# Attention features as sixteen 32x32 TensorE tiles over head pairs, in place of eight 128x64 products

## What is computed

```python
def favor(x, omega):
    dh = x.shape[-1]
    m = 2 * omega.shape[-1]
    xs = x * dh ** (-0.25)
    u = jnp.einsum('bshd,dm->bshm', xs, omega)
    h = 0.5 * jnp.sum(xs * xs, axis=-1, keepdims=True)
    return jnp.concatenate([jnp.exp(u - h), jnp.exp(-u - h)], axis=-1) * m ** (-0.5)
...
q = (out @ Wq[l] + bq[l]).reshape(B, S, N_HEAD, dh)
k = (out @ Wk[l] + bk[l]).reshape(B, S, N_HEAD, dh)
v = (out @ Wv[l] + bv[l]).reshape(B, S, N_HEAD, dh)
Qf = favor(q, omega[l])
Kf = favor(k, omega[l])
a = causal_linear_attention(Qf, Kf, v).reshape(B, S, D)
a = a @ Wo[l] + bo[l]
h = layer_norm(out + a, ln1_g[l], ln1_b[l])
y = jax.nn.relu(h @ W1[l] + bf1[l]) @ W2[l] + bf2[l]
out = layer_norm(h + y, ln2_g[l], ln2_b[l])
```

## Time and profile before

| | |
|---|---|
| median of 3 runs | 2650.11 us (2649.51 to 2653.05) |
| the profiled execution | 2656.85 us |
| its span on the core | 2655.1 us |
| mean granted TensorE clock | 0.989 |
| TensorE busy | 2580.7 us |
| VectorE busy | 2119.8 us |
| ScalarE busy | 1545.6 us |
| GpSimd busy | 1426.2 us |

### The profile page before, as it was taken

One profiled execution on the slowest core, in us unless ns is written; L12 is line 12 of the kernel. 1 busy time (PEld: TensorE's weight loads), 2 busy tenths in 40 slices (PEclk: granted clock), 3 DMA queues, 4 the chain that ended last, 5 costly groups with the idle time before them and its releaser, 6 DMA issues.

```text
span 2655.1 us, 61404 instructions
## 1 busy us (share of the span) xinstructions
PE 2580.7 (97%) x21288; PEld 2131.3 (80%) x21288; DVE 2119.8 (80%) x5244; ACT 1545.6 (58%) x3137; POOL 1426.2 (54%) x1406
## 2 busy tenths in 40 slices
PE   7899999999999999999898999999999999999998
PEld 4688888888888888888786788888888887888886
DVE  5688877787677777888899888888898887888775
ACT  3454445444554455444446777777767777777772
POOL 2253443444343345444476766666666666776664
PEclk9899999999999999999999999999999999999999
DMA  3100000010000010000111000000110110110001
GB/s 93 33 17 10 17 2 17 9 35 6 1 1 8 12 31 25 18 17 26 47 50 52 29 12 19 16 14 19 31 35 23 34 35 22 35 32 26 27 29 48
DMA packets 78976, 67.17 MB, mean 25 GB/s; under 512 B 15800, under 2 KB 73272, under 8 KB 78680
## 3 DMA queue, kind: packets, MB, share of 16 engines
q1 hardware_dynamic: 78680, 63.25, 8.1%
HBM read 49.18 MB, written 12.58 MB: 23 GB/s over the span
## 4 chain that ended last, share of the span: by engine, by line
PE 91%; DVE 3%; issue 2%; ACT 1%; POOL 1%; SPq 0%; DMA 0%; DVEq 0%; ACTq 0%; POOLq 0%
PE PS L274 81%; PE PS L982 4%; PE PS L944 1%; PE PS L935 1%; PE PS L1012 1%; PE PS L487 1%; PE PS L425 1%; PE PS L477 1%; PE PS L893 1%; DVE PS L3583 1%; PE PS L1042 0%; ACT PR L2244 0%; DVE U L3175 0%; DVE SM L3556 0%; DVE SQ L3563 0%
## 5 line engine op out<-in xcount | busy, mean ns | idle before, releaser
L2244 ACT ACTIVATE PR<-PS,SM 128x256 f32<-128x256 f32 (+1 forms) x512 | 280.3, 559 | 137.2 <-DVE SM L3588 136.8
L1930 ACT ACTIVATE FB<-PS,BC 128x512 f32<-128x512 f32 x192 | 133.4, 695 | 326.5 <-PE PS L274 188.0
L3175 DVE TENSOR_TENSOR U<-PS,CST 128x512 f32<-128x512 f32 x384 | 238.2, 683 | 42.1 <-PE PS L274 41.7
L4615 POOL TENSOR_TENSOR RL<-FB,RH 128x512 fp32r<-128x512 f32 x96 | 126.1, 1313 | 236.0 <-DVE RH L3153 236.0
L274 PE MATMUL PS<-W2H,RH 128*128 128x256 f32 x768 | 226.0, 294 | 6.9 <-POOL RL L4615 6.9
L4837 POOL TENSOR_TENSOR SM<-SM,COL 128x8 f32<-128x8 f32 x128 | 225.6, 1763 | 10.7
L3583 DVE CUSTOM_DVE_ANT_0 PS<-PS,MSK 128x256 f32<-128x256 f32 (+1 forms) x512 | 202.6, 436 | 30.0 <-PE PS L274 28.9
L274 PE MATMUL PS<-W2H,RL 128*128 128x256 f32 x768 | 215.8, 281 | 0.0
L274 PE MATMUL PS<-W2L,RH 128*128 128x256 f32 x768 | 215.6, 281 | 0.0
L4627 POOL TENSOR_TENSOR SBD<-SBD,TMP 128x256 f32<-128x256 f32 x84 | 64.5, 768 | 217.2 <-DVE TMP L3167 217.2
L274 PEld LDWEIGHTS PS<-W2H,RH 128*128 128x128 f32 x768 | 145.1, 189 | 29.6 <-issue 25.0
(11 more groups left out here) (265 smaller groups left out, 8711.2 us busy)
## 6 DMA issues: line engine op xcount, KB each, us to landing
PX<-in_L_attn_x SPq DMA_DIRECT2D x16, 512.0 KB, 4.0
TB<-in_k_rot SPq DMA_DIRECT2D x64, 128.0 KB, 2.3
SG<-in_L_attn_W SPq DMA_DIRECT2D x24, 256.0 KB, 2.7
xp_scratch<-PX SPq DMA_DIRECT2D x8, 512.0 KB, 2.9
xs_scratch<-X SPq DMA_DIRECT2D x64, 64.0 KB, 1.5
ZS<-xs_scratch SPq DMA_DIRECT2D x16, 256.0 KB, 2.8
GG<-xp_scratch SPq DMA_DIRECT2D x7, 512.0 KB, 3.7
out<-GG SPq DMA_DIRECT2D x7, 512.0 KB, 2.9
```

Of the source, the lines that this page charges most:

```text
L1930: e.activation(FB[:, hb % 2, :], PS[:, 5, :], ACT.Relu, bias=BC[:, l % 2, 4 + hb:5 + hb]).then_inc(*a_re.up(n, hb))
L2244: t = e.activation(PR[:, par, 256 * i + lo:256 * i + hi], PS[:, 3 + par, 256 * i + lo:256 * i + hi], ACT.Exp, bias=S[:, 40 + 2 * g + i:41 ...
L3175: e.tensor_tensor(heads(U[:, u % 6, :], 4), heads(PS[:, g, :], 4), bcast(CM, 4), ALU.mult).then_inc(*d_mk.up(n, u))
L4615: e.tensor_tensor(RL[:, r, :], FB[:, 0, :], RH[:, r, :].bitcast(F), ALU.subtract).then_inc(*p_rl.up(n, hb))
```

## The change

The columns of Wq and Wk are laid down in another order when they are split, so that `proj(n,i)` yields, in bank i, four bands of 32 partitions: Q of half 0, Q of half 1, K of half 0, K of half 1, each for head pair i of the half. `operands(n,i)` becomes two activations over all 128 partitions: values into A, squares into B (no longer mixed). The bias columns come in the same bands, with 13 DMAs per layer. A visit is one function: 16 products of 32 x 32 with the signed omega block (band r of operand c goes to partitions 32 c of bank r), then 16 of 32 x 32 with the constant -0.125 block on the squares, added in the same banks. It waits for all four operands and both `add_bv`. `values(n,1)` is put ahead of `up` (and of `down`) in chunk 0, in chunk 3 and in the loop. `OM` needs 32 columns and one POOL operation.

```diff
+    BANKS = (2, 3, 0, 1)
...
-    p_om = ev("p_om", by(range(3), R2))
+    p_om = ev("p_om", by(range(3)))
...
-    s_bb = ev("s_bb", by(range(3), range(11)), 16)
+    s_bb = ev("s_bb", by(range(3), range(13)), 16)
...
+        if phase == 1 and at < 1024:
+            def places(w, k):
+                return w[:, 512 * k:512 * k + 512].rearrange("p (s t m f) -> p t m s f", s=4, t=2, m=2)[:, at // 512, :, :, :]
+            return [(places(WQH, k), places(WQL, k), s[:, 256 * k:256 * k + 256].rearrange("p (m s f) -> p m s f", m=2, s=4)) for k in range(2)]
...
         def proj(n, i):
-            m, nm = i % 2, "wk" if i < 2 else "wq"
             if n > 0:
                 e.wait_ge(*d_am.at(n - 1, 1))
-            need_weights(e, piece_of(n // 8, nm))
+            if i == 0:
+                need_weights(e, piece_of(n // 8, "wq"))
+                need_weights(e, piece_of(n // 8, "wk"))
             for k in range(2):
...
-                t = mm3(e, PS[:, i, :], [a[:, 256 * k + 128 * m:256 * k + 128 * m + 128] for a in wt(nm, 0, 512)], xt(0, k, 0, 512), k == 0)
+                t = mm3(e, PS[:, i, :], (WQH[:, 512 * k + 128 * i:512 * k + 128 * i + 128], WQL[:, 512 * k + 128 * i:512 * k + 128 * i + 128]), xt(0, k, 0, 512), k == 0)
...
-        def favor(n, i, bank):
+        def favor(n):
             l = n // 8
-            e.wait_ge(*p_om.at(l, 1))
-            e.wait_ge(*a_sq.at(n, i))
-            if i < 2:
-                e.wait_ge(*a_sq.at(n, 2 + i))
-            else:
-                e.wait_ge(*d_v.at(n, i - 2))
-            mm(e, PS[0:64, bank, :], OM[:, l % 2, 0:64], OPS[i][0], True)
-            mm(e, PS[64:128, bank, :], OM[:, l % 2, 64:128], OPS[i][1], True).then_inc(*e_fv.up(n, i))
+            e.wait_ge(*p_om.at(l))
+            for i in range(4):
+                e.wait_ge(*a_sq.at(n, i))
+            for i in range(2):
+                e.wait_ge(*d_v.at(n, i))
+            for r in BANKS:
+                for c in range(4):
+                    mm(e, PS[32 * c:32 * c + 32, r, :], OM[32 * r:32 * r + 32, l % 2, 0:32], OPS[c][0][32 * r:32 * r + 32, :], True)
+            for i, r in enumerate(BANKS):
+                for c in range(4):
+                    t = mm(e, PS[32 * c:32 * c + 32, r, :], HO[32 * r:32 * r + 32, 0:32], OPS[c][1][32 * r:32 * r + 32, :], False)
+                t.then_inc(*e_fv.up(n, i))
...
             values(n, 0)
             down(m, 0)
+            values(n, 1)
             up(m, 2)
             down(m, 1)
-            values(n, 1)
-            favor(n, 0, 2)
-            favor(n, 1, 3)
-            favor(n, 2, 0)
-            favor(n, 3, 1)
+            favor(n)
             up(m, 3)
...
         def operands(n, i):
-            l, m = n // 8, i % 2
-            lo, hi = slice(0, 64), slice(64, 128)
-            col = BC[:, l % 2, (2 if i < 2 else 0) + m:(2 if i < 2 else 0) + m + 1]
+            l = n // 8
+            col = BC[:, l % 2, i:i + 1]
...
             A, B = OPS[i]
-            e.activation(A[lo, :], PS[lo, i, :], ACT.Identity, bias=col[lo, :])
-            e.activation(B[hi, :], PS[hi, i, :], ACT.Identity, bias=col[hi, :])
-            e.activation(A[hi, :], PS[lo, i, :], ACT.Square, bias=col[lo, :])
-            e.activation(B[lo, :], PS[hi, i, :], ACT.Square, bias=col[hi, :]).then_inc(*a_sq.up(n, i))
+            e.activation(A, PS[:, i, :], ACT.Identity, bias=col)
+            e.activation(B, PS[:, i, :], ACT.Square, bias=col).then_inc(*a_sq.up(n, i))
...
         def features_of(l):
...
-            om = OM[:, l % 2, :].rearrange("p (a f) -> p a f", f=8)
...
-            e.tensor_tensor(om, SG.rearrange("p (a f) -> p a f", f=8), bcast(OMT[:, l % 2, :], 16), ALU.mult).then_inc(*p_om.up(l, 0))
-            e.wait_ge(*p_om.at(l, 0))
-            e.tensor_tensor(OM[:, l % 2, :], OM[:, l % 2, :], HO, ALU.add).then_inc(*p_om.up(l, 1))
+            om = OM[:, l % 2, 0:32].rearrange("p (a f) -> p a f", f=8)
+            e.tensor_tensor(om, SG[:, 0:32].rearrange("p (a f) -> p a f", f=8), bcast(OMT[:, l % 2, :], 4), ALU.mult).then_inc(*p_om.up(l))
...
             for i, nb in enumerate(("bq", "bk")):
-                e.dma_start(BC[:, L, 2 * i:2 * i + 2], ins["L0_attn_" + nb][l].rearrange("(k p) -> p k", p=128), allow_slow_non_contiguous=True).then_inc(*s_bb.up(l, i))
+                for m in range(2):
+                    r = 64 * i + 32 * m
+                    e.dma_start(BC[r:r + 32, L, 0:4], ins["L0_attn_" + nb][l, 128 * m:128 * m + 128].rearrange("(s p) -> p s", p=32), allow_slow_non_contiguous=True).then_inc(*s_bb.up(l, 2 * i + m))
...
-    other = (((i[:, None] + 64) % 128) // 16 == i[None, :] // 16).astype(f) * f(-0.125)
-    cst = np.stack([np.eye(128, dtype=f), blk, other, (i[:, None] <= i[None, :]).astype(f), blk * sign[None, :]], axis=1)
+    pairs = (i[:, None] % 32 // 16 == i[None, :] % 32 // 16).astype(f)
+    cst = np.stack([np.eye(128, dtype=f), blk, pairs * f(-0.125), (i[:, None] <= i[None, :]).astype(f), pairs * sign[None, :]], axis=1)
```

More of the change, by code:

```diff
@@ L612, in _ @@
         values(0, 0)
+        values(0, 1)
         modulate(4)
         modulate(5)
[L615 to L619, removed]
+        favor(0)
         turn_k(0, 0)
@@ L638, in _ @@
         values(1, 1)
[L639 to L642, removed]
+        favor(1)
         attn_out(0, 0)
@@ L669, in _ @@
         up(0, 2)
[L670 to L673, removed]
+        favor(2)
         up(0, 3)
@@ L708, in _ @@
         values(3, 0)
+        values(3, 1)
         up(1, 2)
[L710 to L714, removed]
+        favor(3)
         up(1, 3)
@@ L754, in _ @@
         up(2, 3)
[L755 to L758, removed]
+        favor(4)
         attn_out(3, 0)
@@ L796, in _ @@
         up(3, 3)
[L797 to L800, removed]
+        favor(5)
         attn_out(4, 0)
@@ L1116, in _ @@
         down(20, 1)
[L1117 to L1120, removed]
+        favor(22)
         up(20, 3)
@@ L1158, in _ @@
         down(21, 1)
[L1159 to L1162, removed]
+        favor(23)
         up(21, 3)
@@ L1891, in operands @@
         def operands(n, i):
-            l, m = n // 8, i % 2
-            lo, hi = slice(0, 64), slice(64, 128)
-            col = BC[:, l % 2, (2 if i < 2 else 0) + m:(2 if i < 2 else 0) + m + 1]
+            l = n // 8
+            col = BC[:, l % 2, i:i + 1]
             if i == 0:
-                e.wait_ge(*s_bb.at(l, 10))
+                e.wait_ge(*s_bb.at(l, 12))
             if i == 0 and n > 0:
@@ L5271, in load_columns @@
                 e.wait_ge(*a_re.at(7, 7))
-                e.wait_ge(*p_om.at(1, 1))
+                e.wait_ge(*p_om.at(1))
             for i, nb in enumerate(("bq", "bk")):
-                e.dma_start(BC[:, L, 2 * i:2 * i + 2], ins["L0_attn_" + nb][l].rearrange("(k p) -> p k", p=128), allow_slow_non_contiguous=True).then_inc(*s_bb.up(l, i))
-            e.dma_start(BC[:, L, 4:12], ins["L0_attn_bf1"][l].rearrange("(k p) -> p k", p=128), allow_slow_non_contiguous=True).then_inc(*s_bb.up(l, 2))
+                for m in range(2):
+                    r = 64 * i + 32 * m
+                    e.dma_start(BC[r:r + 32, L, 0:4], ins["L0_attn_" + nb][l, 128 * m:128 * m + 128].rearrange("(s p) -> p s", p=32), allow_slow_non_contiguous=True).then_inc(*s_bb.up(l, 2 * i + m))
+            e.dma_start(BC[:, L, 4:12], ins["L0_attn_bf1"][l].rearrange("(k p) -> p k", p=128), allow_slow_non_contiguous=True).then_inc(*s_bb.up(l, 4))
             for h in range(8):
-                e.dma_start(OMT[16 * h:16 * h + 16, L, :], ins["L0_attn_omega"][l]).then_inc(*s_bb.up(l, 3 + h))
+                e.dma_start(OMT[16 * h:16 * h + 16, L, :], ins["L0_attn_omega"][l]).then_inc(*s_bb.up(l, 5 + h))
         def load_piece(p):
```

## The result

The changed kernel takes 2660.28 us (median of 5 runs, 2658.89 to 2666.34); the kernel before took 2650.17 beside it (5 runs). The ratio is 1.004, 95% interval 1.0026 to 1.0055: slower by 0.4%. The forecast was 2626, in a range from 2607 to 2647, with a chance of 0.82 for faster. It was wrong in sign and in range.

The account below looks back on a forecast made before the run. PE, busy 97% of the span, was taken as the bound. Regular chunks' 15 x 1.35 = 20.3, plus 4.0, minus 0.3 gave 24 us off the median 2650.11: 2626, range 2607 to 2647.

Parts of the forecast that it names:

- the moved wait: Whole visit, not favor(n,3) alone, waits for add_bv(n,1); in regular chunks that ends half a microsecond before the visit.
- regular chunk: Chunk where DVE is ready and idles for PE before add_bv; 15 in all, each gaining 1.35 us.
- `attention` goes earlier too: On ACT, attention moves earlier since values(n,1) is moved ahead, beside halved operands saving 5.6 us per chunk; no size given.
- the late chunks: Chunks where DVE is late by itself: visit starts 0.9 to 1.4 us late; 10, 18, 21 gain about 0.25 each.
- The array: PE's feature matmuls: sixteen tiles at once, a visit of 2.0 us instead of 3.59, saving 1.59, bounds 0.9 and 1.74.
- four at a time: Rival: only four of sixteen tiles work at once, a visit takes 6.9 us, total 2729; chance 0.10.
- Feed: Rival: PE takes 47 instructions per us, a visit is 2.7 us, gain 13, total 2637; chance 0.18.
- Behind the visit: After the visit, PE waits for ACT's release for up(7,4); about 0.2 us given back, a regular chunk gains 1.35.
- Chunks 0 to 5: Gains: chunk 0 nothing, chunk 1 2 us, chunk 2 0.85, chunk 3 nothing, chunks 4 and 5 regular at 1.35.
- small parts: Split Wq and Wk gathers and added DMA issues at the start, less one POOL operation: 0.3 us lost.
- the gain is given back: Rival: visit waits for DVE in every chunk, exponentials hold later work; 0.2 us kept a chunk, total 2645; chance 0.10.
- The sum: Whole kernel: 20.3 us from regular chunks plus 4.0 from others minus 0.3, 24 us gained.

Follow-up runs that it names:

- Experiment 2: Changed kernel, with GpSimd's two X0L subtractions held until add_bv(n,1) is done in chunks 6 to 21: 2643.94 us, ratio 0.9972.
- experiment 1: Changed kernel, with add_bv(n,1) moved ahead of the weight splits and norm2_b(n-3) in the loop of DVE's list: 2636.79 us, ratio 0.9951.
- before_again: The kernel before, unchanged, run once more for a second profile: 2651.22 us, profiled span 2649.4.
- experiment 8: Changed kernel, add_bv earlier on DVE in the loop and chunks 1, 3, 23, ACT's attention behind relu(n-2,2) in the loop: 2626.22 us, ratio 0.9909.

## Why the prediction was wrong

**The step that failed is the moved wait.** It says that "in a regular chunk DVE is ready", from the 1.38 us that DVE idled before its `add_bv` in the earlier trace rows, and that this would end half a microsecond before the visit. DVE had indeed finished the shift in time, in a trace where X0L ran after the visit began. The same part of the prediction notes that "`attention` goes earlier too", and gives it no price; what follows `attention` on GpSimd, X0L, was not looked at. Beside X0L an operation of the shift takes up to 1.5 us instead of 0.48. With 1.04 added to the shift `add_bv` ends 0.6 late instead of half a microsecond early. That an operation can be so long was to be read in the trace of before, where three of the 64 were (one in chunk 4, two in chunk 6) and PE did not wait for them (ns shortest/median/longest of the same operation there):

```profile
L3022 DVE SCALAR_TENSOR_TENSOR X<-Z,ST,BB x64: 472/479/1521, 185.6 to 999.0; 128x256 f32<-128x256 f32 x64
```

The Trainium skill has a rule for this, in "SBUF — State Buffer", "Who interferes with whom": VectorE and GpSimd share a pair of SBUF ports under an exclusive lock, a VectorE instruction with two SBUF inputs contends with a GpSimd instruction that reads SBUF, and the order of issue decides who is blocked. The trace agrees: the shift reads Z and BB, X0L reads NUM and X0H. X0L's first operation starts at 504.81 and takes 1.42; the whole 1.04 falls on the one shift operation that starts behind it, at 505.00, and takes 1.52, while the other three take 0.48 each. `add_bv`, which reads one operand from PSUM, runs beside X0L's second operation in its usual 0.74. Experiment 2 shows the cause, not the port; that it is the port is the skill's reading.

**In the late chunks** the prediction put `add_bv` 0.9 to 1.4 us after the visit's old start. It took the place of `add_bv` on DVE from the earlier trace rows as fixed. But the same contention lengthens the steps in front of it. DVE and GpSimd of the changed kernel, chunk 10:

```profile
558.84 1.52 DVE L3022 CAST W2H<-SG 128x512 fp32r<-128x512 f32 x1
560.29 2.67 DVE L3002 SCALAR_TENSOR_TENSOR X<-Z,ST,BB 128x256 f32<-128x256 f32 x4
562.88 0.74 DVE L3165 TENSOR_TENSOR VP<-PS,BB 128x256 f32<-128x256 f32 x2
...
558.48 3.01 POOL L4597 TENSOR_TENSOR X0L<-NUM,X0H 128x512 fp32r<-128x512 f32 x2 [0.24 <-ACT X0H L1924]
```

1.1 us on the cast and 1.0 on the shift: 2.1 of the pause of 3.35 (experiment 2 leaves 1.5 of it). Chunks 11 and 20 had been counted as regular and paused 1.9 and 2.5 us. In chunk 11 both operations of X0L fall on the shift, which takes 3.73; with X0L held back (experiment 2) chunk 11 does not pause and chunk 20 only 0.5.

**The clock** took a little more. PE idled 3.35 us ahead of the visit of chunk 10, and right behind that its granted clock was 0.54, near the 1.2 GHz level (the same columns as the earlier trace rows):

```profile
565.00:568.50 3.50, 3.50 (x36) 1.67 (x27) 1.34 (x2) 2.06 (x4) 0.00 (x0) 0.54 0.45 50
...
997.00:1000.50 3.50, 3.50 (x70) 1.85 (x66) 0.79 (x2) 1.45 (x3) 0.00 (x0) 1.00 0.78 198
```

So 3.5 us of matmuls did the work of 1.9, 1.6 us lost. The same is seen in chunk 23 (0.57 from 1275 to 1279), in 6 (0.60 from 346 to 350) and in 21 (0.70 from 1161 to 1165). But the second row is from behind the longest pause of all, 3.4 us ahead of the visit of chunk 18, and the clock stayed at 1.00 there. So a pause of that size was followed by the lower clock in most chunks and not in all; what decides it is not shown. The prediction had no such term, having no pause of that size.

**The array: right in kind, mis-sized in the term.** Sixteen at a time, 0.43 apart, as forecast. The visit is 2.27 us, not 2.0, inside the bounds 1.85 to 2.7. What was mis-sized is the step from the omega products to the squares: in the last tile it takes 0.73 (507.90 to 508.63) instead of 0.43, and the work behind starts 0.52 after that tile's last pass (509.08 to 509.60). The omega tiles had their weights within 0.17 us of loads (the last starts at 507.47); of the squares' loads all but one begin at 508.19 or later, and the squares start as these go through, over 0.44 us instead of 0.11. That the loads hold them up is my reading; no run separates it. Saved: 3.58 - 2.27 = 1.31 a visit instead of 1.59. This takes 6.7 of the 24 us. The rival *four at a time* is out, and so, for these tiles, is the page's rule that led there ("TensorE: Matmul & The Clock Gate" of the Trainium skill, "The mechanism"): tiles of one row group start 7 ns apart in these records, each with its own weight loads, so that loads for a row group begin while a product of the same row group runs. *Feed* is out as a bound too: 128 instructions in 2.27 us are 56 per us, above the 47 of the earlier trace rows.

**Behind the visit: right.** `up(7,4)` begins 514.97 - 507.33 = 7.64 us after the visit's start; before it was 521.34 - 512.57 = 8.77. So 1.13 of 1.31 is kept there, 0.18 given back for 0.2 forecast, and without pauses a regular chunk's period is 52.67 or 53.12 (experiment 1) against 53.82 or 54.27: 1.15 gained, 1.35 forecast. The first exponential follows 2.18 after the visit's start (1.9 to 2.0 forecast).

**Chunks 0 to 5.** 4.5 us were gained up to the visit of chunk 5, near the 3.9 that the prediction has (0.85, 2 and 1.35, less 0.3). That is in part luck: 5.0 of them come between the visits of chunks 1 and 2, where `before_again` had a granted clock of 0.57 from 80 to 84 and 0.50 from 94.5 to 97.5, and the changed kernel 1.00 in both. The small parts were as forecast: the first visit starts 0.2 us later. But 4 and 5 were counted as regular and are not: there `attn_out` follows the visit at once and waits for the exponentials, 3.18 us from the visit's start to the next work against 3.65 and 3.58 before.

**The sum.** Forecast 24 gained. Measured: 24 x 1.31 = 31 of visits, less about 5 given back behind them (0.15 in 21 chunks, 0.4 saved instead of 1.3 in 4 and 5), less 27.2 of waits: -1. The lower clock behind the pauses of chunks 6, 10, 21 and 23, at up to 1.6 each, makes it about -7, and the traces differ by 8.2 (the medians by 10.1). This closes better than its terms are known: chunk 0, forecast at nothing, lost 0.3 (4.94 us from the visit's start to the next work before, 5.24 now) and so has no 1.31 to give, and the low clock of `before_again` in chunks 1 and 2 cost that trace some 3 us. The waits were foreseen for seven visits with some 7.5 us, and came in nineteen with 27. With them gone (experiment 8) the gain is 25.2 us, so the other terms were nearly right in sum. The rival that had the right wait was *the gain is given back*: but it left 0.2 us a chunk, and had no price for contention or clock, so it ended at 2645 instead of above 2650. No rival reached a slower kernel by that way.

## What to carry to other kernels

When a wait is moved to the front of a block of work, follow back the whole list of the engine that releases it, and price each step in it beside the neighbours that it will have after the change, not those in the trace: here two operations of GpSimd came to stand beside the four that mattered. Look at the shortest and the longest of one operation; here a factor of three between them was a collision that nobody depended on yet. A change that makes one block cheaper and gates it on more releasers is tried together with the reordering of their lists: the same matmuls cost 10 us in the old order and gained 25 in a new one.

## What the runs showed that was not expected

- A VectorE operation of 128x256 with two SBUF inputs goes from 0.48 us to 1.5 beside a 128x512 subtraction of GpSimd, a cast of 128x512 from 0.42 to 1.52; making GpSimd wait gained 16 us.
- Sixteen 32x32 fp32 tiles start 7 ns apart, four of them in each row group, and their second passes 0.43 us later. Going from the first set of products to the second, which adds in the same banks, takes 0.73 instead of 0.43 in the last tile.
- The same 32 products in the order omega, squares, omega, squares take 3.97 us instead of 2.27.
- Pauses of PE of 2.7 to 3.35 us (chunks 6, 10, 21, 23) were followed by stretches at a granted clock of 0.54 to 0.70; one of 3.4 us (chunk 18) and those of 0.6, 1.9 and 2.5 us (chunks 9, 11 and 20) were not, and their visits took 2.27.
- The order of DVE's list and the contention cost nothing in a regular chunk without each other: with `add_bv` first the shift is slower still (867 ns on average against 783) and no visit waits.
